# Two issuing queues instead of one for the opening loads of a two-layer attention, spiking-FFN and mixture-of-experts kernel

## The reference, cut to what matters

```python
x = x + L0_ffn(L0_cond(x, mask1, ...))      # x: 64 sequences x 64 positions x 256 features
x = x + L1_ffn(L1_cond(x, fside, mask0, ...))

def L0_cond(x, mask, g_norm, Wq, Wkv, q_scale, k_scale, null_kv, null_attn_bias, w0, b0, g0, w1, b1, g1, w2, b2, Wout, g_out):
    xn = ln(x, g_norm)
    q = (xn @ Wq).reshape(b, n, 16, 64).transpose(0, 2, 1, 3)
    kv = xn @ Wkv                            # one key and one value head
    k, v = kv[..., :64], kv[..., 64:]        # a null key and a null value are put ahead
    q = l2norm(q) * q_scale;  k = l2norm(k) * k_scale
    sim = einsum('bhid,bjd->bhij', q, k) * 8
    # relative-position network: a small MLP over the 127 distances
    pos = arange(-n + 1, n)[:, None]
    h = silu(ln(pos @ w0 + b0, g0));  h = silu(ln(h @ w1 + b1, g1));  bias = (h @ w2 + b2)[idx]
    sim = where(causal or masked, -max, sim + bias)
    return ln(softmax(sim) @ v @ Wout, g_out)

def L0_ffn(x, W_fc, W_proj):                 # squared relu, then 5 steps of a spiking neuron
    y = square(relu(x @ W_fc.T)) @ W_proj.T
    ...
def L1_ffn(X, ...):                          # 4-head attention, then 8 experts (top 2) and a shared one
    ...
```

## Time and profile before

| what | us |
| --- | --- |
| median of 3 runs | 1664.65 |
| the profiled execution | 1665.29 |
| its span, first to last instruction | 1663.3 |
| TensorE busy in the span | 1377.2 |
| VectorE busy | 1247.8 |
| ScalarE busy | 910.1 |
| GpSimd busy | 916.9 |
| bytes moved | 63.70 MB |

### The profile page before, as it was taken

How to read it: one execution, slowest core, us unless ns; L and a number is a source line. 1 busy time by engine, 2 the same in 40 slices (tenths; PEclk the granted TensorE clock), 3 DMA queues, 4 the chain that set the end, 5 groups by cost and what they waited for, 6 DMA issues and landing times.

```text
span 1663.3 us, 40014 instructions
## 1 busy us (share of the span) xinstructions
PE 1377.2 (83%) x13102; PEld 1146.1 (69%) x13103; DVE 1247.8 (75%) x2457; ACT 910.1 (55%) x1960; POOL 916.9 (55%) x900
## 2 busy tenths in 40 slices
PE   1688888888868888868999999976899449999994
PEld 1476767666657777756787787764788337888883
DVE  3599999999953989998877777765887498454457
ACT  1466666666635565644555555544787336444544
POOL 1588788887734454543344344336887212777723
PEclk9699999999998999988999999988999679999997
DMA  7300000000003000001000000001000502332345
GB/s 187 80 7 5 6 5 5 5 5 6 4 6 73 1 1 0 1 2 25 6 6 6 5 6 6 5 6 45 15 13 15 162 27 77 98 97 93 93 153 173
DMA packets 89527, 63.70 MB, mean 38 GB/s; under 512 B 50799, under 2 KB 84338, under 8 KB 89459
## 3 DMA queue, kind: packets, MB, share of 16 engines
q1 hardware_dynamic: 82546, 44.98, 9.9%
q0 software_dynamic: 6912, 17.84, 3.5%
HBM read 39.18 MB, written 18.35 MB: 35 GB/s over the span
## 4 chain that ended last, share of the span: by engine, by line
PE 38%; DVE 7%; ACT 5%; issue 4%; POOL 1%; DVEq 0%; ACTq 0%; POOLq 0%
PE psQ L2003 8%; PE psW L1750 6%; PE psQ L1707 5%; PE psW L1985 4%; ACT oT L855 2%; PE psS L1722 2%; PE psS L1765 2%; PE psT L1684 2%; PE psM L1977 1%; PE psT L1993 1%; PE psW L1865 1%; PE psW L1917 1%; DVE both L1647 1%; PE psM L1695 1%; PE psQ L1932 1%
## 5 line engine op out<-in xcount | busy, mean ns | idle before, releaser
L642 POOL TENSOR_TENSOR pn<-ex,rden 128x1024 f32<-128x1024 f32 x64 | 121.9, 1905 | 298.6 <-DVE rden L1223 298.6
L1750 PE MATMUL psW<-wout,oT 128*128 128x256 f32 x1536 | 209.6, 291 | 33.2 <-ACT oT L855 19.5
L1750 PEld LDWEIGHTS psW<-wout,oT 128*128 128x128 f32 x1536 | 192.0, 194 | 49.6 <-ACT oT L855 29.9
L1707 PE MATMUL psQ<-wq,xT 128*128 128x512 f32 x768 | 201.0, 413 | 0.0
L2003 PE MATMUL psQ<-W,exT 128*128 (+1 forms) x624 | 171.7, 411 | 0.1
L1707 PEld LDWEIGHTS psQ<-wq,xT 128*128 128x128 f32 x768 | 147.7, 199 | 29.8
L692 POOL TENSOR_TENSOR hT<-hf,hT 128x512 fp32r<-128x512 f32 x64 | 100.3, 1568 | 116.6 <-ACT hT L923 116.1
L849 ACT ACTIVATE ex<-ex 128x1040 f32<-128x1040 f32 x64 | 68.5, 1071 | 137.3 <-DVE ex L1194 137.3
L1173 DVE TENSOR_TENSOR ex<-psS,masked_bias 128x1024 f32<-128x1024 f32 x64 | 78.4, 1224 | 83.4 <-PE psS L1765 71.8
L655 POOL TENSOR_TENSOR masked_bias<-bias_t,negmask 128x1024 f32<-128x1024 f32 x64 | 139.6, 2182 | 0.2
L2003 PEld LDWEIGHTS psQ<-W,exT 128*128 128x128 f32 x624 | 110.4, 190 | 19.1 <-issue 0.4
(11 more groups left out here) (296 smaller groups left out, 3673.2 us busy)
## 6 DMA issues: line engine op xcount, KB each, us to landing
both<-results SPq DMA_DIRECT2D x16, 512.0 KB, 8.9
raw_w<-W SPq DMA_DIRECT2D x27, 256.0 KB, 5.1
vv<-vp SPq DMA_DIRECT2D x256, 16.0 KB, 1.8
xf<-xf_all SPq DMA_DIRECT2D x4, 1024.0 KB
out<-X SPq DMA_DIRECT2D x8, 512.0 KB, 2.9
X<-x SPq DMA_DIRECT2D x1, 3584.0 KB, 16.1
raw_q<-Wq SPq DMA_DIRECT2D x2, 1024.0 KB, 6.7
bvv<-v_all SPq DMA_DIRECT2D x128, 16.0 KB, 1.8
```

The source lines that it names most:

```text
L642: nc.gpsimd.tensor_tensor(pn[:], ex[:, :, 0:S], rden[:].unsqueeze(2).to_broadcast([P, H, S]), ALU.mult).then_inc(sem("t_pn"), 1)
L1707: mm = nc.tensor.matmul(psQ[:, half, :], xT[u][:, k, :], wq[w][:, k, half * 512:half * 512 + 512], start=(k == 0 and j == 0), stop=(k == K ...
L1750: mm = nc.tensor.matmul(psW[:, 0:D], oT[u][:, c, :], wout[w][:, c, :], start=(u == 0 and c == 0 and w == 0), stop=(u == 1 and c == CH - 1))
```

## The change

The loads of `raw_q`, `raw_kvn`, `raw_o`, of the small network (eight loads) and of the two halves of the mask leave SP's list. ScalarE issues them, at the head of its own list, in that order; the masks are the last two of thirteen. SP keeps X, the small rows, and the scales. `load_layer` is split in two, and for the second layer both halves are called one behind the other, so that the second layer's order is the old one. All counts and waits stay as they were: VectorE still waits for all 17 loads of `l_loaded` first.

```diff
+            def load_rest(L):
+
+                ld = sem("l_loaded")
                 for b in range(2):
                     sp.dma_start(mask_w[b * S:(b + 1) * S, :, :], ...
@@
-            for name, key in (("w0", "rw0"), ("b0", "rb0"), ("g0", "rg0"), ("b1", "rb1"), ("g1", "rg1")):
-                sp.dma_start(r_rows[name][:], a[key]....to_broadcast([P, D])).then_inc(sem("rel_loaded"), 16)
-            sp.dma_start(r_w1[:], ...).then_inc(sem("rel_loaded"), 16)
-            sp.dma_start(r_w2[:], ...).then_inc(sem("rel_loaded"), 16)
-            sp.dma_start(r_b2[:], ...).then_inc(sem("rel_loaded"), 16)
             sp.dma_start(X[:, 4:TILES, :], x_dram[:, 4:TILES, :]).then_inc(sem("x_in1"), 16)
@@
             load_layer(LAYERS[1])
+            load_rest(LAYERS[1])
@@ at the head of the scalar engine's list
+            ld = sem("l_loaded")
+            nc.scalar.dma_start(raw_q[:], a[LAYERS[0]["wq"]]...).then_inc(ld, 16)
+            nc.scalar.dma_start(raw_kvn[:, :, 0:2 * DH], a[LAYERS[0]["wkv"]]...).then_inc(ld, 16)
+            nc.scalar.dma_start(raw_o[:], a[LAYERS[0]["wo"]]...).then_inc(ld, 16)
+            for name, key in (("w0", "rw0"), ("b0", "rb0"), ("g0", "rg0"), ("b1", "rb1"), ("g1", "rg1")):
+                nc.scalar.dma_start(r_rows[name][:], a[key]....to_broadcast([P, D])).then_inc(sem("rel_loaded"), 16)
+            nc.scalar.dma_start(r_w1[:], ...).then_inc(sem("rel_loaded"), 16)
+            nc.scalar.dma_start(r_w2[:], ...).then_inc(sem("rel_loaded"), 16)
+            nc.scalar.dma_start(r_b2[:], ...).then_inc(sem("rel_loaded"), 16)
+            for b in range(2):
+                nc.scalar.dma_start(mask_w[b * S:(b + 1) * S, :, :], ...).then_inc(ld, 16)
```

More of the change, by code:

```diff
@@ L796, in _ @@
         def _(act):
+            ld = sem("l_loaded")
+            nc.scalar.dma_start(raw_q[:], a[LAYERS[0]["wq"]].rearrange("(k p) n -> p k n", p=P)).then_inc(ld, 16)
+            nc.scalar.dma_start(raw_kvn[:, :, 0:2 * DH], a[LAYERS[0]["wkv"]].rearrange("(k p) n -> p k n", p=P)).then_inc(ld, 16)
+            nc.scalar.dma_start(raw_o[:], a[LAYERS[0]["wo"]].rearrange("(k p) n -> p k n", p=P)).then_inc(ld, 16)
+            for name, key in (("w0", "rw0"), ("b0", "rb0"), ("g0", "rg0"), ("b1", "rb1"), ("g1", "rg1")):
+                nc.scalar.dma_start(r_rows[name][:], a[key].rearrange("(o d) -> o d", o=1).to_broadcast([P, D])).then_inc(sem("rel_loaded"), 16)
+            nc.scalar.dma_start(r_w1[:], a["rw1"].rearrange("(k p) n -> p k n", p=P)).then_inc(sem("rel_loaded"), 16)
+            nc.scalar.dma_start(r_w2[:], a["rw2"].rearrange("(k p) n -> p k n", p=P)).then_inc(sem("rel_loaded"), 16)
+            nc.scalar.dma_start(r_b2[:], a["rb2"].rearrange("(h o) -> h o", o=1), allow_slow_non_contiguous=True).then_inc(sem("rel_loaded"), 16)
+            for b in range(2):
+                nc.scalar.dma_start(mask_w[b * S:(b + 1) * S, :, :], a[LAYERS[0]["mask"]].rearrange("(t b) j -> b t j", b=2)[b:b + 1]
+                             .to_broadcast([S, TILES, S // 4])).then_inc(ld, 16)
             def split_hi(L):
```

## The result

The changed kernel takes 1679.92 us, the median of 4 runs (1678.22 to 1681.13), against 1664.56 us (1664.33 to 1665.13): the ratio is 1.0094, interval 1.0081 to 1.0107. It is slower by 15.4 us. The forecast was 1670.4 in a range of 1661.5 to 1675.0: the direction came out, and so did the load that is waited for, but the size is more than twice the 5.7 us forecast, and outside the range. The profiled execution took 1680.22 us. Three executions in the comparisons further down (one of the kernel before, one of masks_own, one of one_queue) took 1989 us or more, and the times given leave them out.

A forecast was written before the change was run, and what follows sets the result against it. The prediction took the chain of starting loads that releases VectorE as the bound: T of 27.0 less 21.3 costs +5.7 us, span 1663.3 to 1669.0, median forecast 1670.4 us, range 1661.5 to 1675.0.

The forecast's parts named there:

- A shift of the chain passes to the end one for one: Kernel start: everything hangs behind the load chain, so a later or earlier start moves the end by the same time.
- L1262's wait of 0.48 us goes away, so the cost is T - 21.3: Small network's first instruction: no wait for r_b2, so it runs at T + 7.1 against 28.38 before.
- T: Time when the last of l_loaded's 17 loads has landed and VectorE starts: 20.8 us before, forecast 27.0.
- The sum of the engines' work: DMA engines' work for the starting loads: 29.1 us in all, 17.9 without the rest of X.
- With the engines shared evenly: ScalarE's queue beside the rest of X: 9.1 us of work left takes 18.2; T 25 to 30, chance 0.52.
- this rule: DMA engines alternate between queues by packet, so 64-byte mask pieces wait for X's 1 KB pieces: T about 28 to 30.
- T is 2.2 + 29.1 + 0.7 = 32.0: Upper bound of VectorE's start: the rest of X goes entirely before the masks, T 32.0 us.
- the 2.7 us for the network's rows: Small network's rows leave engines free for other traffic: 2.6 us of work instead of 5.3, taking T from 29.9 to 27.2.
- ScalarE's issues from 0.8 to 7.9, the rest of X at about 8.5: Issue at the start: ScalarE's thirteen issues take some 7.1 us at no cost; X's rest comes at 8.5 instead of 22.18.
- The fourth rival, X first: ScalarE's issues stall, masks reach the engines behind the rest of X: T 30 to 32, +9 to +10.7 us, chance 0.10.

The follow-up runs named there:

- masks_own: The changed kernel with the masks on a semaphore of their own, waited for only ahead of the instruction that reads them: 1667.44 us.
- one_queue: The kernel before, all loads on SP, with the two mask loads moved behind r_b2, just ahead of the rest of X: 1670.00 us.
- masks_first: The changed kernel with the two mask loads at the head of ScalarE's list instead of its end: 1669.73 us.
- best_one: The kernel before, still one queue, reordered with null_key's loads first; masks, raw_o and some rows under a second semaphore: 1713.09 against 1718.56 us.
- before_again: The kernel before, unchanged, measured against itself: 1664.54 against 1664.63 us.
- masks_mid: The changed kernel with the masks between the weights and the small network on ScalarE's list: 1675.47 us.
- x_behind: The changed kernel, but SP waits for the 17 loads of l_loaded before issuing the rest of X: 1667.94 us.
- masks_wide: The changed kernel with the same mask bytes in 2 KB pieces (128) instead of 64-byte pieces (4096): 1727.90 against 1718.56 us for the kernel before.
- best_two: As best_one, but ScalarE issues raw_q, raw_kvn and the small network, and SP the other loads: 1662.38 against 1664.63 us for the kernel before.

## Why the prediction was wrong, step by step

**"A shift of the chain passes to the end one for one": right.** From VectorE's start to the first matmul there are 13.15 us before (20.80 to 33.95) and 13.15 after (35.12 to 48.27). From there to the end it is 1629.4 before (1663.3 - 33.95) and 1630.0 after. In the profiles of the first and third group this remainder lies between 1627.6 and 1631.3, so of the 15.0 us of span 14.3 are the start and 0.7 is within this spread. The medians follow the start less closely: the time moves by up to 2.8 us more than the start to the slower side (masks_first 5.3 for 2.5, with an interval of 3.8 to 7.8), and by 1.5 less than it in best_one. What this surplus is stays open; before_again shows that it is not in the comparison.

**"L1262's wait of 0.48 us goes away, so the cost is T - 21.3": wrong by 0.5.** The wait went away and gained nothing. What stands between null_key and the first matmul is ScalarE: in the kernel before its table load starts when null_key ends and its SiLU 5.4 us later, and the small network's vector work ran beside that.

```profile
27.98 1.28 ACT L803 ACT_TABLE_LOAD   x1 [27.98 <-DVE raw_kvn L1126]
33.39 0.42 ACT L813 ACTIVATE r_h<-r_h 128x256 f32<-128x256 f32 x1
```

After, the same two rows are at 42.30 and 47.70. The price is T - 20.8, with T = 35.1: 14.3 us.

**T, the term that was mis-sized: 27.0 forecast, 35.1 measured.** The sum of the engines' work was near (27.8 measured, 29.1 forecast), and that the masks come behind more work and beside X was right. Two things in it failed, and the sum has a slip.

- "With the engines shared evenly", the 9.1 us of work left take twice their time: this step failed. From 22 to 26 us, with both queues at work, X's pieces took 96.5% of the engines' time and the masks' 19.8%, while in pieces it was 1239 to 1053 (1149 to 1077 in masks_mid). At 1053 in 4 us the 4096 pieces of mask take 15.6 us, an estimate, where twice their 3.9 us of work is 7.8; the 7.8 us between the two are about the size of the miss of 8.1. Two runs bear on it: without X the masks' queue moves 3624 pieces in 4 us and VectorE starts at 22.9, and the same bytes in larger pieces are 7.5 us earlier. One for one is no rule of all stretches, though (967 to 1457, 1256 to 380, and 1020 to 105 with 2 KB pieces). The Trainium skill, DMA: Bandwidth & Descriptors, section Queues, rings and completion order, has each engine take turns between queues a packet of several descriptors at a time. The trace agrees in the two stretches named, in that there a 64-byte and a 1 KB piece count alike; it doesn't show packets, and the other stretches don't follow from the rule alone. The prediction had this rule beside its sum, and put T at 28 to 30 by it, which was still too early by 5 us.
- "T is 2.2 + 29.1 + 0.7 = 32.0" was the upper bound and held only if the engines never idle. They were at 0.69 from 13 to 22 us, while small rows and the network's rows went on, and at 0.53 from 30 to 35, where the ends of X and of the masks thin out. This is 2.8 + 2.3 = 5.1 us of idle time. In x_behind they are at 0.69 from 13 to 22 too, without X, so the idle time there doesn't need X; that the slow spread rows or the issue cause it is likely and not tested. A bound made of work alone was no bound.
- A slip in the sum: the 2.7 us for the network's rows are taken off after the doubling. Taken off the work first, it is 11 + 2 x 6.4 + 0.7 = 24.5, further still from 35.1.

**"ScalarE's issues from 0.8 to 7.9, the rest of X at about 8.5": wrong.** The masks were issued from 11.97 to 24.1 and the rest of X at 11.69. Issue durations are no constant: the rest of X took 0.43 us to issue before and 1.61 now, the two masks 1.98 before, 12.16 now, and 8.55 in x_behind, where no X is beside them. It cost ScalarE nothing, as forecast, since it was idle until 42.30.

**The parts.** The order alone is +4.4 us of start (one_queue). The second queue with the rest of X kept behind is -2.3 us (x_behind against one_queue). The rest of X let in beside the masks is +12.2 us. They add up to 14.3, as they must, being differences between neighbouring starts. In time one_queue and x_behind, on one chip, are 2.1 us apart. Without the masks in the count it would be +2.3 (masks_own). The fourth rival, X first, at 1674.5 and a chance of 0.10, was nearest in its time, though not in its mechanism: neither went first.

**Open:** why the masks moved slowly from 18 to 22 us in masks_mid; where the 4.7 us of masks_wide over x_behind go; and the surplus of up to 2.8 us of time over start.

## What to carry to other kernels

Look first at what a shared count makes wait: a load that is needed late must not be in the count that releases the first instruction, or must stand first in its queue. A second queue removes the order between its loads and the other's, so a bulk load that used to be safely behind now competes with everything; keep it behind by a wait, above all where small pieces are still under way. A bound from the engines' work needs the idle time of the same trace added. Where two queues count into one semaphore, check the name of the last load against the sizes of the pieces that still move: in masks_mid the profile's name was the wrong one.

## What the runs showed of the hardware that was not expected

- With both queues full, 64-byte and 1 KB pieces went about one for one: 1239 pieces of 1 KB beside 1053 of 64 bytes in 4 us in the changed kernel, 1149 beside 1077 in masks_mid. It was not so in every stretch (967 to 1457 in the changed kernel from 26 to 30 us), nor with 2 KB pieces (1020 to 105 in masks_wide).
- An issue can hold its engine for long: 12.16 us for two loads of 2048 pieces each in the changed kernel, 14.35 in masks_mid, 8.55 in x_behind, 6.87 with the weights beside them, 1.98 in the kernel before.
- A load of 1 KB in 4-byte pieces took 3.7 us from issue to landing in the kernel before, and 11.7 in best_two, with the weights and the network's rows on the other queue.
- The chip of the second group ran the kernel before in 1718.56 us, 54 us more than the two others.
